# A decoder layer between attention and gate/up: the low parts of transposed rows come from PSUM on VectorE, and both rounding steps of quantised rows move to GpSimd

## The reference: what is computed

```python
q = jnp.clip(jnp.round(x / s + z), 0.0, 255.0)      # fake_quant(x, s, z)
return (q - z) * s
...
x = _layernorm(x + jnp.matmul(fake_quant(x, ...), fake_quant(ctx, ...)))
```

## Time and profile before

| | |
|---|---|
| time, median of three runs | 1514.62 us |
| the profiled execution, its own time | 1513.12 us |
| its span (what the trace covers) | 1511.3 us |
| busy, share of the span: PE, DVE, ACT, POOL | 97%, 63%, 48%, 42% |
| the stage of this change | about 1024 to 1126 us of the span |

### The profile page before, as it was taken

The page is one execution under the profiler, slowest core; times in us unless marked ns, Lnnn a source line. Parts: engine busy times, 40 slices in busy tenths (PEclk is TensorE's granted clock), DMA queues, the critical chain, the costliest instruction groups (busy, mean ns, idle before and its releaser), DMA issues.

```text
span 1511.3 us, 23061 instructions
## 1 busy us (share of the span) xinstructions
PE 1470.4 (97%) x7501; PEld 1205.1 (80%) x7501; DVE 946.1 (63%) x1691; ACT 721.9 (48%) x1440; POOL 627.9 (42%) x566
## 2 busy tenths in 40 slices
PE   7999999999999999999999999999799999999996
PEld 6788888888878888888888888887478888888642
DVE  7644444445566677777877777776744444444597
ACT  5433333333444465666666665654752222222564
POOL 0477777776566454555555555543630000000000
PEclk9999999999999999999999999999999999999998
DMA  6477777777652857666676757660102221222111
GB/s 222 159 276 276 276 275 275 274 275 268 216 191 91 313 191 250 228 235 222 226 246 215 260 187 275 202 223 1 56 1 96 99 104 69 104 79 94 50 42 71
DMA packets 103572, 272.66 MB, mean 180 GB/s; under 512 B 12512, under 2 KB 12896, under 8 KB 103520
## 3 DMA queue, kind: packets, MB, share of 16 engines
q1 hardware_dynamic: 103520, 272.02, 51.5%
HBM read 180.75 MB, written 91.23 MB: 180 GB/s over the span
## 4 chain that ended last, share of the span: by engine, by line
PE 60%; DMA 3%; DVE 3%; ACT 2%; issue 2%; POOL 1%; SPq 0%; ACTq 0%; DVEq 0%; POOLq 0%
PE ps L1116 10%; PE ps L1115 10%; PE ps L938 7%; PE ps L939 6%; PE ps L940 6%; PE ps L1123 5%; PE ps L889 2%; PE ps L890 2%; PE ps L891 2%; PE ps L920 2%; PE ps L921 2%; PE ps L1023 1%; PE ps L902 1%; PE ps L919 1%; DMA f_raw<-w_gu 1%
## 5 line engine op out<-in xcount | busy, mean ns | idle before, releaser
L1115 PE MATMUL ps<-xt_h,w_h 128*128 128x512 f32 x672 | 262.0, 390 | 0.0
L1116 PE MATMUL ps<-xt_l,w_h 128*128 128x512 f32 x672 | 261.5, 389 | 0.0
L870 PE MATMUL ps<-xo_h,wb_h 128*128 128x512 f32 x644 | 251.7, 391 | 7.5 <-issue 6.0
L871 PE MATMUL ps<-xo_l,wb_h 128*128 128x512 f32 x644 | 251.3, 390 | 0.0
L872 PE MATMUL ps<-xo_h,wb_l 128*128 128x512 f32 x644 | 251.1, 390 | 0.0
L938 PE MATMUL ps<-wo_h,o_h 128*128 128x512 f32 x512 | 206.3, 403 | 0.0
L939 PE MATMUL ps<-wo_l,o_h 128*128 128x512 f32 x512 | 199.8, 390 | 0.0
L940 PE MATMUL ps<-wo_h,o_l 128*128 128x512 f32 x512 | 199.6, 390 | 0.0
L1762 POOL TENSOR_TENSOR pm_l<-pt_l,upto 128x512 fp32r<-128x512 f32 x64 | 82.5, 1288 | 250.6 <-DVE pt_l L2001 250.6
L870 PEld LDWEIGHTS ps<-xo_h,wb_h 128*128 128x128 f32 x644 | 121.2, 188 | 34.0 <-issue 9.1
L1115 PEld LDWEIGHTS ps<-xt_h,w_h 128*128 128x128 f32 x672 | 126.2, 188 | 26.4
(11 more groups left out here) (188 smaller groups left out, 3126.1 us busy)
## 6 DMA issues: line engine op xcount, KB each, us to landing
raw<-w_att SPq DMA_DIRECT2D x47, 512.0 KB, 5.5
f_raw<-w_gu SPq DMA_DIRECT2D x44, 512.0 KB, 5.0
w_h<-u_gu SPq DMA_DIRECT2D x43, 512.0 KB, 4.0
u_gu<-f_unit SPq DMA_DIRECT2D x42, 512.0 KB, 4.5
wp_raw<-w_att SPq DMA_DIRECT2D x32, 512.0 KB, 5.9
wo_high<-wp_h SPq DMA_DIRECT2D x32, 512.0 KB, 2.8
wo_low<-wp_l SPq DMA_DIRECT2D x32, 512.0 KB, 4.1
q_rows<-c SPq DMA_DIRECT2D x64, 256.0 KB, 2.9
```

The source lines that it names most:

```text
L870: pe.matmul(prod_ps[i], wh, chunk(xo_h[i], c), start=(i in OPENS and c == 0), stop=False, skip_group_check=True)
L871: pe.matmul(prod_ps[i], wh, chunk(xo_l[i], c), start=False, stop=False, skip_group_check=True)
L1115: pe.matmul(dst, w, xt_h[:, c, rows], start=(c == 0), stop=False)
L1116: last = pe.matmul(dst, w, xt_l[:, c, rows], start=False, stop=(c == DC - 1))
```

## The change

`columns_whole` and `x2_whole` go. `columns_high` signals `x2_copied`. VectorE makes the low part of every tile, at the end of its slot, from the two banks and `xt_h`. `turn_x2(t)` now waits for `x2_low` of tile t-1, since VectorE is the last to read the banks. The first rounding step moves from the end of VectorE's slot to GpSimd, right ahead of the second, which still waits for its semaphore. GpSimd makes no low parts any more.

```diff
 # TensorE, turn_x2(t)
                 pe.wait_ge(ln_done[1], t + 1)
-                wait(pe, x2_copied, t)
+                wait(pe, x2_low, t)
 # ScalarE
             def columns_high(t):
                 act.activation(xt_h[:, :, t * P:(t + 1) * P], ps[:, 2:4, :].rearrange("p a (c q) -> p (a c) q", q=P),
-                               ACT.Copy)
-
-            def columns_whole(t):
-
-                wait(act, x2_low, t)
-                act.activation(x2_whole[:, :, :], ps[:, 2:4, :].rearrange("p a (c q) -> p (a c) q", q=P),
                                ACT.Copy).then_inc(x2_copied, 1)
...
-                if 5 <= i < TILES + 5:
-                    columns_whole(i - 5)
 # GpSimd
             def quantise_rows(t):
+                pool.wait_ge(x_scaled_done, t + 1)
+                pool.tensor_scalar(x_scaled[:, t % 2, :], x_scaled[:, t % 2, :], QMAX, ROUND, ALU.min,
+                                   ALU.add).then_inc(x_rounded, 1)
                 pool.wait_ge(x_rounded, t + 1)
...
             def slot(i):
-                if 6 <= i < LOW_BY_POOL + 6:
-
-                    rows = slice((i - 6) * P, (i - 5) * P)
-                    pool.wait_ge(x2_copied, i - 5)
-                    pool.tensor_tensor(xt_l[:, :, rows], x2_whole[:, :, :], xt_h[:, :, rows].bitcast(F32),
-                                       ALU.subtract).then_inc(x2_low, 1)
 # VectorE
-            def round_rows(t):
-                dve.wait_ge(x_scaled_done, t + 1)
-                dve.tensor_scalar(x_scaled[:, t % 2, :], x_scaled[:, t % 2, :], QMAX, ROUND, ALU.min,
-                                  ALU.add).then_inc(x_rounded, 1)
-
...
                 dve.wait_ge(x2_copied, t + 1)
                 rows = slice(t * P, (t + 1) * P)
-                dve.tensor_tensor(xt_l[:, :, rows], x2_whole[:, :, :], xt_h[:, :, rows].bitcast(F32),
+                dve.tensor_tensor(xt_l[:, :, rows], ps[:, 2:4, :].rearrange("p a (c q) -> p (a c) q", q=P),
+                                  xt_h[:, :, rows].bitcast(F32),
                                   ALU.subtract).then_inc(x2_low, 1)
...
-                if 1 <= i < TILES + 1:
-                    round_rows(i - 1)
-                if LOW_BY_POOL + 5 <= i < TILES + 5:
+                if 5 <= i < TILES + 5:
                     columns_low(i - 5)
```

More of the change, by code:

```diff
@@ L37 @@
 QMAX = 255.0
-LOW_BY_POOL = 6
 CENTRE = 128.0
@@ L170, in build @@
         x_q = place("x_q", [P, 2, DM], BF16, at_t + 8192)
-        x2_whole = place("x2_whole", [P, DC, P], F32, at_t + 20480)
         ctx_sum = place("ctx_sum", [P, BATCH, DM], F32, at_r4 + 32768)
@@ L1842, in _ @@
             slot(3)
-            for i in range(4, max(LOW_BY_POOL + 6, TILES + 3)):
+            for i in range(4, TILES + 3):
                 if i < TILES + 2:
```

## The result

The changed kernel takes 1517.66 us (median of 18 runs, 1514.12 to 1519.44), the kernel before 1514.28 us (median of 18, 1509.34 to 1518.11). The ratio is 1.0019, 95% interval [1.0012, 1.0027]. A second measurement of both gave 1.0029 [1.0018, 1.0040]. I had forecast 1512.8 us, in a range that ended at 1515.1.

What follows compares the result with a forecast made beforehand. TensorE's waits on ScalarE's list in slots 6 to 9 were taken as the bound. Removing x_whole twice, 2 x 0.91 = 1.82 us, with other terms 0, took 1514.62 us to 1512.8 us, range 1509.6 to 1515.1.

Steps and rivals of the forecast that it cites:

- The place that bounds the stage: Slots 6 to 9: TensorE waits 10.0 us for ScalarE's list, with x_whole, 0.91 us, twice on the chain.
- the sum: x_whole leaves ScalarE's list in slots 6 and 8: 2 x 0.91 = 1.82 us less, all other terms 0.
- Edit 2: VectorE makes the low part from PSUM at 1.28 us; delay of the chain 0, at most +0.4 us.
- Edit 4: GpSimd does both rounding steps, the first at 1.12 us, far bound 2.35 us; term 0, at most +1.0 us.
- The cover that I claimed in slots 2 to 5: Slots 2 to 5: a tile's attention products lie ahead of the quantised rows' transpose and cover its lateness; term 0.
- rival B: GpSimd or VectorE takes up what ScalarE gives back: both new steps at 2.35 us, 1514.2 us; chance 0.07.
- Edit 5: Slots 7 and 9: both clock falls stay, after waits of 3.7 and 3.5 us; term 0, at best -3.0 us.
- signs of being wrong: A TensorE wait on xt_l or x_q, clock 1.00 in slot 7 or 9, or a rounding step above 1.8 us.
- C: Clock falls in all four slots, with three falls in the gate/up products: +3.1 us, 1517.7 us; chance 0.03.
- Edit 3: First rounding step leaves VectorE: in slot 6 cross_add(3) starts 0.5 us earlier, turn_x2(3) 1.4 us earlier; term 0.
- the odd loop: Odd tiles' loop (slots 6, 8), interleaved with the even tiles' (slots 7, 9), which ends last; term 0.
- the four gaps of the earlier trace: TensorE's waits in slots 6 to 9: 1.34, 3.72, 1.05, 3.91 us; clock falls after the two long ones only.

Runs made afterwards that it cites:

- Extra copy: Changed kernel with the first rounding step back on VectorE, plus an unread 128x768 copy on ScalarE in x_whole's place: 1513.80 us, 0.9998 of the kernel before.
- round on VectorE: Changed kernel with the first rounding step back on VectorE, behind the low part: 1511.15 us, 0.9975 of the kernel before; run again 1511.29 us, 0.9980.
- part 2: Not a run: the trace window from the load for the first transpose of turn_x2(0) to that for the first gate/up product (slots 5 to 9).
- no clip: Changed kernel whose first rounding step on GpSimd multiplies by 1.0 and adds, without the clip at 255: 1511.35 us, 0.9980 of the kernel before; step 1.04 us.
- second profile: The changed kernel, unaltered, measured once more: median 1518.70 us, 1.0029 of the kernel before.
- first probe: Kernel before plus 16 one-input instructions on a free tile at the end of GpSimd's stage; min+add took 3.6 us, no kernel time given.
- the last experiment: Rounding and low part both on VectorE, with the rounding ahead of the low part: 1513.41 us, 0.9990 of the kernel before.
- rounding alone: Kernel before with only the first rounding step moved to GpSimd, x_whole and GpSimd's low parts kept: 1524.04 us, 1.0062 of the kernel before.
- tiles 0, 1 on VectorE: Changed kernel with the first rounding step of tiles 0 and 1 back on VectorE: 1515.23 us, 1.0012 of the kernel before; again 1515.61 us, 1.0008.
- tiles 0 and 1 alone on GpSimd: Changed kernel with the first rounding step of tiles 2 to 7 back on VectorE, behind the low part: 1515.59 us, 1.0001 of the kernel before.
- part 1: Not a run: the trace window from the load for the first attention output product behind the context's sums to that for turn_x2(0)'s first transpose (slots 2 to 5).

## Why the prediction was wrong, step by step

- **The place that bounds the stage** was right: ScalarE's list, twice on the chain. Extra copy takes the gain away, round on VectorE gives 1.89 us of part 2 for the 1.82 of the sum.
- **Edit 2, the low part on VectorE,** was right: 1.22 us for the 1.28 I took, and no wait for it.
- **Edit 4 failed, and it is the step of the miss.** I priced the first rounding step at 1.12 us, with 2.35 us as "the far bound"; it takes 3.63. The bound was none. I had looked for the nearest row by engine, width, type and number of inputs, and not by operation: every GpSimd row with two scalars was mult followed by add, a pair that happens to be quick. The new step was min followed by add. Of the kernel before, no row showed that form on GpSimd, and I should have left its upper end open. The sentence of the Trainium skill that I leaned on ("GPSIMD Engine Reference", "Engine selection": one-input operations at about line rate) holds for 3 of the 14 forms tried; the measurement decides against it for the others.
- **The cover that I claimed in slots 2 to 5** was short. Attention products do lie ahead of those transposes, but the rows of tiles 0 and 1 were ready only 2.0 and 1.7 us before they were needed (kernel before, timelines: x_q done at 1038.4 and 1044.7, transposes at 1040.5 and 1046.5). The step takes 2.9 us more than on VectorE (3.63 for 0.69). In slot 2 that makes 0.83 us of waiting; in slot 3 another 1.08, since the step of tile 1 also stood behind GpSimd's own context addition of tile 0 (its start, 1043.34, is the end of that). TensorE was full there, so nothing gives it back: 2.2 us, at full clock. I gave this cover a sentence and no number.
- **Slots 6 to 9.** At full clock the dear step costs there what rival B's formula says. From the end of a `cross` of the even loop to the transposes of x_q in the next slot it is 12.14 us in the changed kernel and 10.26 us in "no clip" (slot 7): 1.88 us for 2.51 too much less 0.7 of slack. Both slots together give 3.6 - 1.8 = +1.8 us. The +0.22 us measured are less because of the clock: the kernel before worked at half of it for 3.4 us in slot 7 and 3.4 us in slot 9, both on the path. The changed kernel did so in slot 7, where 0.45 us of it were a wait, and in slot 8, where TensorE then waited for x_q all the same. Half speed over work costs half of its time, so 3.4 us for the one kernel and 1.5 for the other. Taken out, that leaves an estimate of 0.2 + 1.9 = +2.1 us. The second profile against the first probe gives the same, 1.7 + 0.3. With slots 2 and 3 it makes 4.3 us; the medians of the two measurements are 3.4 and 4.8 us apart.
- **Edit 5** had both falls of the clock staying, in slots 7 and 9. The changed kernel broke that in its first profile, where slot 9 ran at 1.00, one of the signs of being wrong that I had listed; in its second one they are in slots 7 and 9. So it is luck of the clock that the first profile shows so small a loss in part 2.
- **The rivals.** B was the right mechanism, GpSimd takes up what ScalarE gives back, with the wrong price. Its break-even of 2.8 us was never run, and it counts slots 6 to 9 only, with nothing for slots 2 and 3; I gave it 0.07, because "every row of that kind is at 1.1 us". C, to which I gave the slower side, didn't occur: from the first gate/up product to the end the changed kernel takes 406.7 us, the one before 406.9. That C's 1517.7 us is the measured median is chance.
- **Edit 3:** in the kernel with the quick step, `turn_x2(3)` comes as early as I wrote. That the odd loop costs nothing when it is late was wrong, as the last experiment shows.

## What to carry to other kernels

When a step moves to another engine, price it by a row of the same operation there; engine, width and operand count are not enough, and without such a row the upper end is open. Give each claimed cover its slack in us at every place, the first tiles of a pipeline included: there, a late handover on an otherwise full engine is never won back. And where two loops take turns on the same engines, a delay of the one that isn't last can come out in the other. Before two executions are compared, look where the lower clock lay in each: over work on the path, over a wait, or beside the path.

## What the runs showed of the hardware

**GpSimd's one-input f32 step has two speeds**, 1.05 to 1.4 us for three pairs of operations and 2.8 to 4.2 us for the eleven other forms tried, at 128x1024. VectorE does the same min+add in 0.69 us.

**TensorE's lower clock lasts longer in some executions of a program than in others.** Part 2 has two stretches at a clock of 0.50, the lower level, in all profiles but two (one in the second "round on VectorE", three in "rounding alone"). Each lasts about 3.4 or about 6.8 us. Here is one microsecond, 4.4 us behind the start of slot 7, of the kernel before and of the first probe, the same program in this stage:

```profile
1085.43:1086.43 1.00, 1.00 (x7) 0.47 (x5) 0.64 (x1) 1.00 (x2) 0.44 (x1) 1.00 0.00 0
```

```profile
1086.50:1087.50 1.00, 1.00 (x3) 0.30 (x2) 0.64 (x1) 1.00 (x2) 0.43 (x1) 0.50 0.00 0
```

Part 2 by kernel and mean granted clock; both probes are the kernel before there. First one probe (the other has 40.56 us at 0.83 too), then the changed kernel again, then round on VectorE again:

```profile
1066.50:1107.06 40.56, 30.28 (x198) 18.30 (x201) 25.31 (x77) 30.09 (x40) 30.25 (x18) 0.83 0.14 53
```

```profile
1068.50:1110.79 42.29, 31.57 (x202) 17.62 (x201) 28.70 (x78) 25.63 (x35) 33.76 (x18) 0.84 0.13 51
```

```profile
1067.58:1103.12 35.54, 27.08 (x198) 15.79 (x201) 31.10 (x82) 25.18 (x35) 19.09 (x13) 0.95 0.16 60
```

| part 2, us | clock 0.91 | 0.83 or 0.84 | 0.95 |
|---|---|---|---|
| before | 38.93 | 40.56, 40.56 | |
| changed | 39.15 | 42.29 | |
| tiles 0, 1 on VectorE | 39.19 | 42.59 | |
| round on VectorE | 37.04 | 39.60 | 35.54 |
| extra copy | | 40.30 | |

The 39.60 is from the kernel with tiles 0 and 1 alone on GpSimd, which has the same instructions as round on VectorE in part 2.

So one kernel's executions differ by 1.5 to 3.4 us here, and the mean clock doesn't say all: it counts where the stretch lies. In the kernel before both stretches of 3.4 us lie over work on the path. In the first probe 1.2 and 2.2 us of its two stretches of 6.8 us pass while TensorE waits. Half of the time over work is 3.4 and 5.1 us, a difference of 1.7; measured are 40.56 - 38.93 = 1.63 us. For the same reason the gain of round on VectorE is 1.89 us at a clock of 0.91 and only 0.96 at 0.83: with shorter waits, more of a long stretch lies over work (0.7 and 0.9 us of waiting in it instead of 1.2 and 2.2).

By mean clock the changed kernel is +0.22 or +1.73 us in part 2, with part 1 2.4 or 3.9 us in all, 0.16 or 0.26% of 1514 us. The two measured ratios, 1.0019 and 1.0029, are of that size. Why the clock stayed low for longer in one execution than in another of the same program, no run shows. Nor does the length of one wait foretell a fall. In the changed kernel the clock fell in slots 7 and 8, where no wait of TensorE was above 1.84 us, and in "rounding ahead of the low part" it stayed at 1.00 through slot 8, which opened with a wait of 2.10 us. I had taken the four gaps of the earlier trace rows as if their length decided it. Slot 8 of the changed kernel:

```profile
1094.00:1095.00 1.00, 1.00 (x5) 0.40 (x4) 0.86 (x4) 1.00 (x1) 1.00 (x1) 0.70 0.00 0
1095.00:1096.00 1.00, 1.00 (x3) 0.29 (x2) 0.00 (x0) 1.00 (x3) 0.12 (x1) 0.50 0.00 0
```
